# A three-stage transformer layer: broadcasts, down-weight loads and the attention product moved

## The reference

```
def _layernorm(x, axis=-1, eps=1e-5):
    ...
W = (wq.astype(float32) - 128.0) * scale[:, None]      # gate, up: [8192, 2048]; down: [2048, 8192]; int32
h = silu(x @ Wg.T) * (x @ Wu.T);  ffn = h @ Wd.T

q = (x @ Wq + bq).reshape(B, L, GROUPS, HPG, HEAD_DIM)          # 4 groups of 8 heads of 64
kv = (x @ Wkv + bkv).reshape(B, L, GROUPS, 2, HEAD_DIM)
scores = jnp.einsum('blghd,blgd->blgh', q, k)[..., None] / math.sqrt(HEAD_DIM)
attn = jax.nn.softmax(scores, axis=-1)
out = attn * v[:, :, :, None, :]

x = x + 0.5 * ffn(layernorm(x)); x = x + attention(layernorm(x)); x = x + 0.5 * ffn(layernorm(x))
```

## Time and profile before

| | us |
|---|---|
| two timed runs | 7610.1 and 7676.8, median 7643.45 |
| the profiled execution | 6926.7 |
| its span, slowest core (core 3) | 6925.1 |
| spans of the other cores | 6844.5 to 6887.0 |
| mean granted TensorE clock, core 3 | 0.945 of full speed |
| busy: PE, DVE, ACT, POOL | 5830.7, 931.8, 790.1, 488.0 |

### The profile page before, as it was taken

The page is one execution under the profiler, slowest core; times in us unless marked ns, Lnnn a source line. Parts: engine busy times, 40 slices in busy tenths (PEclk is TensorE's granted clock), DMA queues, the critical chain, the costliest instruction groups (busy, mean ns, idle before and its releaser), DMA issues.

```text
span 6925.1 us, 67654 instructions; the slowest of 8 cores (6844.5 to 6925.1 us)
## 1 busy us (share of the span) xinstructions
PE 5830.7 (84%) x26642; PEld 2609.3 (38%) x26642; DVE 931.8 (13%) x1502; ACT 790.1 (11%) x621; POOL 488.0 (7%) x582
## 2 busy tenths in 40 slices
PE   1699679994789989998774569999998799989998
PEld 0344234431334434443332224444443344434443
DVE  0200000001110000002233320000002200000000
ACT  0233303332100000000000000000000000000000
POOL 0000210011100000000120100010000000010001
PEclk9999999997889999999886779999999899999999
DMA  7466877666752265227703142274227522472246
GB/s 148 164 223 215 232 184 239 223 215 183 182 122 76 73 149 134 76 76 180 150 25 73 61 94 76 73 168 125 77 73 182 123 76 76 116 161 77 77 115 155
DMA packets 433659, 909.03 MB, mean 131 GB/s; under 512 B 34883, under 2 KB 266435, under 8 KB 408004
## 3 DMA queue, kind: packets, MB, share of 16 engines
q1 hardware_dynamic: 353702, 642.53, 31.1%
q0 software_dynamic: 72736, 211.85, 14.6%
q10 hardware_dynamic: 6912, 50.33, 2.2%
HBM read 728.16 MB, written 203.69 MB: 135 GB/s over the span
## 4 chain that ended last, share of the span: by engine, by line
PE 74%; DMA 17%; DVE 4%; issue 2%; ACT 2%; another core or an unknown queue 2%; DVEq 0%; POOL 0%; ACTq 0%; SPq 0%; POOLq 0%
PE PS L627 51%; PE PS L762 19%; DMA WD<-dwb 7%; DMA ARF<-dwt 5%; PE PS L912 3%; DMA xo<-ARF 2%; DMA ARF<-xo 2%; DVE ST L386 1%; ACT WD L718 1%; PE PS L881 1%; DVE YT L458 1%; DVE ARF L991 0%; ACT ARF L431 0%; DVE ARF L784 0%
## 5 line engine op out<-in xcount | busy, mean ns | idle before, releaser
L762 PE MATMUL PS<-WD,ARB 128*128 128x512 bf16 x8192 | 1897.9, 392 | 430.0 <-ACT WD L718 213.8
L627 PE MATMUL PS<-YT,WG 128*128 128x512 bf16 x8192 | 1822.2, 381 | 21.0 <-ACT WG L592 11.0
L627 PE MATMUL PS<-YT,WU 128*128 128x512 bf16 x8192 | 1809.9, 379 | 0.0
L762 PEld LDWEIGHTS PS<-WD,ARB 128*128 128x128 bf16 x8192 | 807.2, 100 | 1516.8 <-issue 659.1
L627 PEld LDWEIGHTS PS<-YT,WG 128*128 128x128 bf16 x8192 | 804.2, 98 | 997.3 <-issue 39.5
L627 PEld LDWEIGHTS PS<-YT,WU 128*128 128x128 bf16 x8192 | 801.4, 98 | 966.7
L652 DVE SCALAR_TENSOR_TENSOR ARB<-ARF,CON,PS 128x1024 bf16<-128x1024 f32 x256 | 327.7, 1280 | 3211.3 <-PE PS L627 3211.3
L641 ACT ACTIVATE ARF<-PS,CON 128x1024 f32<-128x1024 f32 x256 | 285.2, 1114 | 3707.4 <-PE PS L627 3707.4
L798 POOL DMA_DIRECT2D xo<-ARF x256 | 223.8, 941 | 4488.1 <-DVE ARF L784 4347.4
L447 PE MATMUL PS<-CON,ARF 128*128 128x128 bf16 x768 | 88.1, 282 | 498.7 <-DVE YT L458 267.0
L784 DVE TENSOR_TENSOR ARF<-PS,ARF 128x512 f32<-128x512 f32 x256 | 177.1, 692 | 2052.8 <-PE PS L762 1709.4
(11 more groups left out here) (42 smaller groups left out, 577.3 us busy)
## 6 DMA issues: line engine op xcount, KB each, us to landing
WD<-dwb SPq DMA_DIRECT2D x896, 256.0 KB, 3.6
WG<-gwb SPq DMA_DIRECT2D x192, 512.0 KB, 3.3
WU<-uwb SPq DMA_DIRECT2D x192, 512.0 KB, 3.3
ARB<-gwt SPq DMA_DIRECT2D x64, 1024.0 KB, 7.2
ARB<-uwt SPq DMA_DIRECT2D x64, 1024.0 KB, 9.5
ARF<-dwt SPq DMA_DIRECT2D x128, 512.0 KB, 5.4
xo<-ARF POOLq DMA_DIRECT2D x256, 256.0 KB, 7.3
ARF<-xo ACTq DMA_DIRECT2D x48, 1024.0 KB, 5.6
```

Of the source, the lines that this page charges most:

```text
L627: wring=wring, soff=soff: E.matmul(dst[:, j * 512:j * 512 + w], wring[:, soff + k * 128: soff + (k + 1) * 128], yt[:, k * TILE + j * 512: ...
L762: jj=jj, tsv=tsv, ic=ic: E.matmul(psd, arb[:, ic * TILE + tsv * 128: ic * TILE + tsv * 128 + 128], wd[:, soff + jj * D4: soff + (jj + 1) * ...
```

## The change

- **Prologue.** The three row loads are issued together (into XS1, XS0 and Y0), one row of ones serves all three, and the order is `bq`, `ds`, `bkv`; the third is spread into XS0 instead of `DSBC`. ACT waits for the stores (`bst`) before its first load.
- **Attention.** The junction is called after the softmax instead of before it, and its list goes into a local `trickle`. The product with v moves from DVE to POOL and goes into `DSBC` and `TMP_OA`. In att1 SP reloads `BKVB`, over which `TMP_OA` lies, after `vkv` and the accumulates, and DVE waits for it. The load of the scaled `ds` into `DSBC` for the second FFN moves from att1's junction to behind att1, and waits for the accumulates.
- **FFN.** In the halves that read bf16 weights the first four chunk loads of `WD` are issued ahead of the gate/up loads of the same half. The junction gets two more entry waits on ACT (`gpr`, `gsr`).

The diff, cut to its core:

```diff
-        bcast_row(d_bq, D, 0, DSBC, None)
...
+        b.op("sync", lambda E: E.dma_start(
+            out=arf[0:1, XS0:XS0 + D], in_=d_dsr), incs=[("cld", 16)], dma=True)
+        b.op("sync", lambda E: E.dma_start(
+            out=arf[0:1, XS1:XS1 + D], in_=d_bq), incs=[("cld", 16)], dma=True)
+        b.op("sync", lambda E: E.dma_start(
+            out=arf[0:1, Y0:Y0 + KVW], in_=d_bkv), incs=[("cld", 16)], dma=True)
...
+        def _bc_build(row_off, width, dst_off, scale, dram_row):
...
+            b.wait("vector", "pbc", b.n("pbc"))
+            if dst_off is not None:
+                b.wait("vector", "bst", b.n("bst"))
...
+        _bc_build(XS1, D, DSBC, None, d_bc[0])
+        _bc_build(XS0, D, DSBC, 0.5, d_bc[1])
+        _bc_build(Y0, KVW, XS0, None, d_bc[2])
...
+                if not is_int:
...
+                    for i, (hq, ch) in enumerate(_chl[:4]):
+                        idx = nch0 + i
...
+                        if idx >= 4:
+                            b.wait("sync", "dpe", idx - 3)
...
+                        b.op("sync", lambda E, src_b=src_b, dstw=dstw:
+                             E.dma_start(out=dstw, in_=src_b),
+                             incs=[(f"dld{slot}", 16)], dma=True)
+                        preload[idx] = b.n(f"dld{slot}")
...
+            if not first:
+                b.wait("sync", "vkv", b.n("vkv"))
+                for sl in range(2):
+                    b.wait("sync", f"aac{sl}", b.n(f"aac{sl}"))
+                b.op("sync", lambda E: E.dma_start(
+                    out=arf[:, BKVB:BKVB + KVW], in_=d_bc[2][:, 0:KVW]),
+                    incs=[("bld", 16)], dma=True)
+                b.wait("vector", "bld", b.n("bld"))
...
-            if junction is not None:
-                b.mark("junc")
-                r = junction()
-                if isinstance(r, list):
-                    for f in r:
-                        f()
...
             b.mark("aoa")
-            b.wait("vector", "sy", b.n("sy"))
+            trickle = []
+            if junction is not None:
+                b.mark("junc")
+                r = junction()
+                if isinstance(r, list):
+                    trickle = r
+            TMP_OA = TMP + 5 * NSUB * GH
...
             for ts in range(NSUB):
-                oslot = XS1 if ts % 2 else XS0
-                b.wait("vector", f"aac{ts % 2}", b.n(f"aac{ts % 2}"))
+                oslot = TMP_OA if ts % 2 else DSBC
+                b.wait("gpsimd", f"aac{ts % 2}", b.n(f"aac{ts % 2}"))
...
-                b.op("vector", lambda E, aview=aview, vview=vview, oslot=oslot:
+                if ts == 0:
+                    b.wait("gpsimd", "vsm", b.n("vsm"))
+                b.op("gpsimd", lambda E, aview=aview, vview=vview, oslot=oslot:
...
+        b.wait("scalar", "pbc", b.n("pbc"))
+        b.wait("scalar", "bst", b.n("bst"))
...
-        attn_phase(1, first=False, junction=f2a_junction)
+        attn_phase(1, first=False, junction=ln_junction(0))
+        for sl in range(2):
+            b.wait("sync", f"aac{sl}", b.n(f"aac{sl}"))
+        b.op("sync", lambda E: E.dma_start(
+            out=arf[:, DSBC:DSBC + D], in_=d_bc[1][:, 0:D]),
+            incs=[("bld", 16)], dma=True)
```

More of the change, by code:

```diff
@@ new lines, in build_program @@
+        b.op("sync", lambda E: E.dma_start(
+            out=arf[0:1, XS1:XS1 + D], in_=d_bq), incs=[("cld", 16)], dma=True)
+        b.op("sync", lambda E: E.dma_start(
+            out=arf[0:1, Y0:Y0 + KVW], in_=d_bkv), incs=[("cld", 16)], dma=True)
+        b.op("vector", lambda E: E.memset(
+            arf[0:1, TMP:TMP + 128], 1.0), incs=[("von", 1)])
+        b.wait("tensor", "cld", b.n("cld"))
+        b.wait("tensor", "von", b.n("von"))
+        ones_ap = arf[0:1, TMP:TMP + 128]
+        def _bc_build(row_off, width, dst_off, scale, dram_row):
+            nmm = (width + 511) // 512
+            b.bank_wait("tensor", range((width + 511) // 512))
+            for j in range(nmm):
+                w = min(512, width - j * 512)
+                b.op("tensor", lambda E, j=j, w=w, row_off=row_off: E.matmul(
+                    ps[:, j * 512:j * 512 + w], ones_ap,
+                    arf[0:1, row_off + j * 512:row_off + j * 512 + w],
+                    start=True, stop=True),
+                    incs=([("pbc", 1)] if j == nmm - 1 else []))
+            b.wait("vector", "pbc", b.n("pbc"))
+            if dst_off is not None:
+                b.wait("vector", "bst", b.n("bst"))
+            if scale is None:
+                b.op("vector", lambda E, width=width, dst_off=dst_off:
+                     E.tensor_copy(arf[:, dst_off:dst_off + width],
+                                   ps[:, 0:width]), incs=[("vbc", 1)])
+            else:
+                b.op("vector", lambda E, width=width, dst_off=dst_off:
+                     E.tensor_scalar_mul(arf[:, dst_off:dst_off + width],
+                                         ps[:, 0:width], scale),
+                     incs=[("vbc", 1)])
+            b.bank_set(range((width + 511) // 512), "vbc", b.n("vbc"))
+            if dram_row is not None:
+                b.wait("sync", "vbc", b.n("vbc"))
+                b.op("sync", lambda E, width=width, dst_off=dst_off,
+                     dram_row=dram_row: E.dma_start(
+                         out=dram_row[:, 0:width],
+                         in_=arf[:, dst_off:dst_off + width]),
+                     incs=[("bst", 16)], dma=True)
@@ L535, in j @@
             def j():
-                extra = [("scalar", "vhh", b.n("vhh"))]
+                extra = [("scalar", "vhh", b.n("vhh")),
+                         ("scalar", "gpr", b.n("gpr")),
+                         ("scalar", "gsr", b.n("gsr"))]
                 return ln_junction_items(tile, yring, extra_waits=extra)
@@ L560, in ffn_phase @@
                 flush_base_prev_half = b.n("vfl")
+                if not is_int:
+                    chunkwb = b.aux.setdefault("dch_wb", {})
+                    preload = b.aux.setdefault("dpre", {})
+                    nch0 = b.n("dch")
+                    _chl = [(hq, ch) for _t in range((NSUB + 3) // 4)
+                            for hq in range(4)
+                            for ch in range(max(1, ICH // 2))]
+                    for i, (hq, ch) in enumerate(_chl[:4]):
+                        idx = nch0 + i
+                        slot = idx % 4
+                        soff = slot * 2 * D4
+                        ics = ([2 * ch, 2 * ch + 1] if ICH >= 2 else [0])
+                        nsl = len(ics)
+                        src_b = d_dwb[half, hq].rearrange(
+                            "(cc p) h -> p cc h", p=128)[
+                            :, ics[0]:ics[0] + nsl, :]
+                        dstw = wd[:, soff:soff + nsl * D4].rearrange(
+                            "p (cc h) -> p cc h", h=D4)
+                        if idx >= 4:
+                            b.wait("sync", "dpe", idx - 3)
+                        wbprev = chunkwb.get(idx - 4)
+                        if wbprev is not None:
+                            b.wait("sync", wbprev[0], wbprev[1])
+                        chunkwb[idx] = None
+                        b.op("sync", lambda E, src_b=src_b, dstw=dstw:
+                             E.dma_start(out=dstw, in_=src_b),
+                             incs=[(f"dld{slot}", 16)], dma=True)
+                        preload[idx] = b.n(f"dld{slot}")
                 for ic in range(ICH):
@@ L729, in ffn_phase @@
                             else:
[L730 to L744, removed]
+                                pre = b.aux.setdefault("dpre", {}).pop(nch,
+                                                                       None)
@@ new lines, in ffn_phase @@
+                                if pre is not None:
+                                    b.wait("tensor", f"dld{slot}", pre)
+                                else:
+                                    if is_int and tq == 1 and hq == 0 \
+                                            and ch == 0:
+                                        for sl in range(4):
+                                            b.wait("sync", f"dwb{sl}",
+                                                   b.n(f"dwb{sl}"))
+                                    if nch >= 4:
+                                        b.wait("sync", "dpe", nch - 3)
+                                        wbprev = chunkwb.get(nch - 4)
+                                        if wbprev is not None:
+                                            b.wait("sync", wbprev[0],
+                                                   wbprev[1])
+                                    chunkwb[nch] = None
+                                    b.op("sync", lambda E, src_b=src_b,
+                                         dstw=dstw: E.dma_start(
+                                             out=dstw, in_=src_b),
+                                         incs=[(f"dld{slot}", 16)], dma=True)
```

(2 more changed lines are left out.)

5 lines of the change are left out of this document (4 added, 1 removed).

## The result

| | before | after |
|---|---|---|
| profiled execution, span of the slowest core | 6925.1 us | 7000.9 us (core 4) |
| median span of cores 0 to 3 | 6877.4 us | 6927.2 us |
| median of all timed runs | 7484.35 us (31 runs) | 7167.69 us (32 runs) |
| lowest to highest of them | 6887.8 to 7987.4 | 6941.5 to 7991.5 |
| **ratio after / before** | | **1.0075, 95% interval 1.005 to 1.0099** |

The changed kernel is 0.75% slower, which is about 52 us at the level of the lowest runs (0.0075 × 6910). The single times of either kernel spread over more than 1000 us, because in many executions the cores of a die show a lower granted clock whatever the kernel is, so the ratio compares only runs without that; the raw medians even point the other way. The forecast had +46 us, and a time of 7689 us in a range from 7610 to 7765. The change is as forecast; the time is not in the range.

The account below looks back on a forecast made before the run. Down matmuls hold TensorE, idle 430.0 us ahead of them, but the change works only in prologue, attention stretches and FFN-half starts; −7 + 14 + 16 + 23 = +46 us, added to 7643.45 gives 7689 us, range 7610 to 7765.

Parts of the forecast that it names:

- The time: Whole kernel: 7689 us, from the timed median 7643.45 plus 46, in a range from 7610 to 7765.
- my own ends: Whole kernel: the forecast difference with all low terms, +8 us, and with all high terms, +68 us.
- The difference: Whole kernel: +46 us on the profiled execution, 6926.7 becoming about 6973; forecast chance 0.77.
- Prologue: Program start: row loads issued together let SP and ACT start earlier, −7 us (ends −8.5 and −5).
- Between the attention tiles: Attention tile 0 to 1: softmax, POOL products with accumulates, then whole layer norm, 167.0 against 153.0 us, +14 (+5 to +18).
- What I gave as its cause: Between attention tiles: the junction's items are never run, so the layer norm runs whole in `ln_full` after every accumulate.
- Into the second FFN: Attention tile 1 to second FFN: same 167.0 plus 8 for SP's 4 MB beside the x load, +16 (0 to +22).
- The chunk loads ahead: Second halves of f1b, f2a, f2b: WG queued behind the fourth chunk's wait, 7.7 us per start, +23 (+12 to +33).
- The other estimate: Chunk loads ahead: 2.0 us plus bytes at 436 GB/s lands 512 KB in 3.2 us; three starts cost 19.
- Rival A: Chunk loads at FFN halves: the preload pays or costs nothing, +23 or −17 in all, 7626 to 7666 us; chance 0.12.
- Rival B: Attention products: POOL slow with both operands broadcast, 11.5 us per product to pass +153 us, 7796; chance 0.05.
- Rival C: Attention stretches: layer norm gets under the products, up to 51 us hidden in each, −56 in all, 7587; chance 0.03.

Follow-up runs that it names:

- e0: The kernel before, unchanged: eight runs have a median of 7684.3 us, sixteen runs of the same program beside them 7252.5 us; no ratio came out.
- e7: The changed kernel with odd products in XS1, so BKVB is not reloaded: first x load 5.1 us on core 3, stretch between tiles 206.8 us against 208.4.
- e9: The changed kernel with the junction's items run ahead of the softmax, as in the kernel before: attention stretches 212.9 and 186.7 us.
- e3: The kernel before with only the chunk loads sent ahead: ratio to the kernel before 1.010 (1.0052 to 1.0148).
- e2: The changed kernel without the chunk loads sent ahead: ratio to the kernel before 1.0044 (1.0014 to 1.0074).
- e4: The changed kernel with the four chunk loads issued behind the first two slab pairs: gaps 0.6 us at most, gate/up blocks 442.0; timing gave no ratio.
- e5: The changed kernel with the junction's items run ahead of the products: ratio to the kernel before 0.9943 (0.9914 to 0.9972), stretches 167.7 and 141.2 us.

## Why the prediction was right or wrong

- **The time, wrong.** The step that failed is the base of the last sum: the median of two timed runs, 7643 us, was taken for the level of the kernel, the +46 was added to it (7689 us), and 33 us were allowed for the spread of a median on either side. The profiled execution beside them was at 6926.7 and was named as 10% away. The runs showed that there is no such level: single executions of the kernel before lie anywhere from 6888 to 7987 us, its median over 31 is 7484, and e0 gives 7684 and 7252 for one program. The changed kernel's median came out at 7168, and the 317 us between the two medians of the result lie within that spread, so a median inside the range would have been luck. The range should have reached from the profiled execution's level, 6935 to 6995 with my own ends, up to the timed ones; I widened it for the sizes of my terms, which were the smaller doubt.
- **The difference, right.** +46 forecast; 45.8 by stage, 1.0075 (about 52 us) by the ratio, its interval from 35 to 68. That 46 and 45.8 agree so closely is luck: the terms below are off by up to 3 us in both directions.
- **Prologue, right**: −7 forecast, −6.9 measured. SP's first load was forecast for 134.2 and came at 134.41, but by two errors that cancel: on this core the rows were there 1.1 us later, and the second store landed 4.1 us behind the DVE copy that fed it, where I had 5.1. ACT's wait for the last store was mis-sized (2 forecast, 5.5); it cost at most 1.6 us, since the x load came through 16.7 us behind the first weight load instead of 15.1.
- **Between the attention tiles, right**: +14 forecast, +15.3 by the medians. The terms on core 3: softmax 5.5 (5.1 forecast), products to the last landing 58.5 (59.4), layer norm from the first load to the first matmul 103.5 (100.9 + 1.3). Two wrong sizes hid each other: the product takes 3.6 us and not 4.5, the landing 8.8 and not 8.0. The reload of `BKVB`, costed at nothing, makes the first x load 2.7 us longer (e7).
- **What I gave as its cause was half of it.** That the layer norm is run whole is seen, and as a form costs nothing. The prediction did say that its entry waits for every accumulate, and counted the last landing, but never set it against the kernel before, where the KV matmuls do not wait for it. On core 3 that wait is 8.9 of the 14.6 us, and the product on POOL, with a longer turn of a slot, 7.0; e9, with the order put back, keeps both steps and is no shorter.
- **Into the second FFN, right within its ends**: +16 forecast, +12.8. The x load was late by 4 us, not 8; no run shows why it is late by less than in the prologue, which I took as the nearest row.
- **The chunk loads ahead, right**: 7.7 us for each start, measured 5.9 idle and 2.3 of clock. Nothing came back in the down stages (e3), and SP's order is the cause (e2, e4). The Trainium skill's rule on waits inside matmul loops (TensorE: Matmul & The Clock Gate, HAM oscillation) holds here: each of the three blocks behind a gap is 2.0 to 2.6 us longer. The other estimate that the prediction sets beside its sum, 19 us by the Trainium skill (DMA: Bandwidth & Descriptors, Anatomy of one DMA), uses a fit that the page gives for DMAs issued from GpSimd; WG is issued by SP, and the sum doesn't use it.
- **Rival A** (preload free) fell by e2 and e3. **Rival B** (POOL slow on the product) fell: 3.65 us is the mean of the 16:

```profile
L1069 POOL TENSOR_TENSOR ARF<-ARF,ARB 128x2048 f32<-128x2048 f32 x16 | 58.4, 3650 | 32.5 <-DMA xo<-ARF 16.5 <-DVE ARF L1042 15.9
```

- **Rival C** (layer norm under the products) did not happen, for the reason given, and e5 shows what it would have been worth: 80 us (40.7 and 39.0), where I had up to 102.

## What to carry to other kernels

A load sent ahead is only ahead of what stands in front of it in its queue; if it carries a wait, everything behind it in that queue gets the wait too, so put it behind the loads that are needed first. Moving work to an idle engine pays only if the busy engine's next work is then issued; look for who now waits for the moved work's last result and didn't before. And before a time is forecast, compare the profiled execution with the timed runs: where they lie 10% apart, forecast the difference from the profile, and let the range of the time span both levels.

## What the runs showed that I had not expected

- POOL's product with v, with both operands broadcast, takes 3.65 us where its product with k, with one of them broadcast, takes 4.50, at the same 128 × 2048 elements. No run varies the operands one by one, so that the broadcast is the reason isn't shown.
- A 1 MB x load takes 5.1 us alone and 7.3 to 9.2 us with a 256 KB load of 128 short rows issued 0.1 us ahead of it (e7 against the changed kernel).
